# A windowed-attention block on one core: FC2 in three float16 products, with gelu's output split on GpSimd

## The reference

```python
f = _ln(x.transpose(0, 2, 3, 1), g1, b1)
f = jnp.roll(f, (-SS, -SS), axis=(1, 2))
q, k, v = split(_window_partition(f) @ w_qkv + b_qkv)
attn = softmax(einsum('bhid,bhjd->bhij', q, k) * scale + mask)
out = einsum('bhij,bhjd->bihd', attn, v) @ w_proj + b_proj
f = residual + roll_back(_window_reverse(out))
m = _ln(f, g2, b2)
m = gelu(m @ w_fc1 + b_fc1, approximate=False) @ w_fc2 + b_fc2
return f + m
```

## Time and profile before

| | |
|---|---|
| median of 3 runs | 2974.03 us (2972.49 to 2977.97) |
| the profiled execution | 2974.94 us, span 2973.1 us |
| mean granted TensorE clock | 0.99 of full speed |
| busy: TensorE, VectorE, ScalarE, GpSimd | 96%, 81%, 69%, 59% |
| DMA | 359.65 MB, mean 121 GB/s |

### The profile page before, as it was taken

The page is one execution under the profiler, slowest core; times in us unless marked ns, Lnnn a source line. Parts: engine busy times, 40 slices in busy tenths (PEclk is TensorE's granted clock), DMA queues, the critical chain, the costliest instruction groups (busy, mean ns, idle before and its releaser), DMA issues.

```text
span 2973.1 us, 141485 instructions
## 1 busy us (share of the span) xinstructions
PE 2851.0 (96%) x54820; PEld 2383.1 (80%) x54820; DVE 2405.7 (81%) x7142; ACT 2036.8 (69%) x3208; POOL 1760.3 (59%) x2088
## 2 busy tenths in 40 slices
PE   3899999999999999999999999999999999999998
PEld 2788888888878888888887888888888788888886
DVE  6788887888888888788887888888888888888885
ACT  1677776677667777667766776767777677777674
POOL 3566566556656556565665566566565566666655
PEclk7999999999999999999999999999999999999999
DMA  3444444444445444444444444444444444444441
GB/s 72 126 123 126 130 121 126 121 125 126 126 118 130 125 129 123 120 125 123 125 129 114 124 127 125 125 123 125 130 122 126 121 124 130 127 121 129 122 113 42
DMA packets 414934, 359.65 MB, mean 121 GB/s; under 512 B 63646, under 2 KB 414176, under 8 KB 414204
## 3 DMA queue, kind: packets, MB, share of 16 engines
q1 hardware_dynamic: 414220, 350.04, 45.1%
HBM read 193.29 MB, written 154.14 MB: 117 GB/s over the span
## 4 chain that ended last, share of the span: by engine, by line
PE 89%; ACT 5%; issue 3%; DVE 2%; SPq 0%; DMA 0%; POOL 0%; DVEq 0%; POOLq 0%; ACTq 0%
PE psum L502 18%; PE psum L484 10%; PE psum L417 8%; PE psum L466 8%; PE psum L528 7%; PE psum L543 6%; PE psum L618 5%; PE psum L619 5%; PE psum L591 5%; PE psum L424 5%; ACT probs L678 4%; PE psum L428 3%; PE psum L581 3%; PE psum L445 2%; PE psum L570 1%
## 5 line engine op out<-in xcount | busy, mean ns | idle before, releaser
L678 ACT ACTIVATE probs<-psum 113x784 f32<-113x784 f32 x768 | 633.0, 824 | 639.1 <-PE psum L484 635.8
L796 DVE TENSOR_REDUCE nmax<-psum 113x16 f32<-113x784 f32 x768 | 745.5, 971 | 152.0 <-PE psum L466 151.6
L380 POOL TENSOR_SCALAR ve<-mv 98x8 f32<-98x8 f32 (+1 forms) x264 | 64.1, 243 | 1118.7 <-DVE mv L825 1085.9
L502 PE MATMUL psum<-vbd,probs 128*49 128x18 f32 x24576 | 642.5, 198 | 3.7 <-issue 3.0
L502 PEld LDWEIGHTS psum<-vbd,probs 128*49 128x49 f32 x24576 | 632.5, 126 | 6.7 <-issue 6.1
L387 POOL TENSOR_TENSOR rs<-ve,half 98x8 f32<-98x8 f32 (+1 forms) x264 | 435.3, 1649 | 0.0
L484 PE MATMUL psum<-qbd,kst 128*49 128x196 f16 x6144 | 401.5, 251 | 32.9 <-DVE xfl L831 21.9
L392 POOL TENSOR_TENSOR xn<-xn,rs 98x768 f32<-98x768 f32 (+1 forms) x264 | 383.3, 1452 | 74.5 <-POOL rs L387 74.5
L820 DVE BATCH_NORM_STATS2 st<-tok 98x6 f32<-98x96 f32 x2080 | 359.5, 246 | 71.3 <-ACT tok L685 56.4
L466 PE MATMUL psum<-kbd,qst 128*49 128x196 f16 x6144 | 399.2, 250 | 10.6 <-DMA kbd<-stack_pages 7.1
L383 POOL TENSOR_TENSOR xn<-tok,mv 98x768 f32<-98x768 f32 (+1 forms) x264 | 384.8, 1458 | 0.6 <-POOL ve L380 0.6
(11 more groups left out here) (90 smaller groups left out, 5716.3 us busy)
## 6 DMA issues: line engine op xcount, KB each, us to landing
stack_pages<-nat SPq DMA_DIRECT2D x256, 294.0 KB, 3.0
kst<-stack_pages SPq DMA_DIRECT2D x256, 220.5 KB
qbd<-stack_pages SPq DMA_DIRECT2D x1024, 55.1 KB
stack_pages<-nat SPq DMA_DIRECT2D x256, 147.0 KB, 2.1
xr<-in_x_dram SPq DMA_DIRECT2D x224, 147.0 KB, 3.2
out_dram<-yr SPq DMA_DIRECT2D x224, 147.0 KB, 2.3
qst<-stack_pages SPq DMA_DIRECT2D x256, 73.5 KB
kbd<-stack_pages SPq DMA_DIRECT2D x1024, 18.4 KB
```

The costliest lines, as they stand in the source:

```text
L502: last = nc.tensor.matmul(dst[:, :, h, :], probs[:, b.c % 2, h // 4, p, h % 4 * L:(h % 4 + 1) * L], vbd[:, b.c % 4, p * NH + h, :, :], sta ...
L678: nc.scalar.activation(probs[0:PR, b.c % 2, u, :, :].rearrange("j (g q) k -> j g (q k)", g=2), psum[0:PR, B:B + 2, 0:2 * CH], ACT.Exp).the ...
L796: nc.vector.tensor_reduce(dst, psum[0:PR, A:A + 2, 0:2 * CH].rearrange("i g (q h j) -> i g q h j", q=2, j=L), axis=AX.X, op=ALU.max, negat ...
```

## The change

FC2 becomes three float16 products for each float32 one: w2 times 64 is split once into w2h and w2l on VectorE (`split_w2`), the output of gelu is split into hidh and hidl for every band on GpSimd (`split_hidden`, a cast and a subtraction), at the head of the even step. FC2's sum, still in banks D, is read by ScalarE (`scaled`, at the end of its even step), which removes the 64 and adds FC2's bias, into a new tile ys in SBUF; VectorE's `result` adds f to ys, no longer to PSUM. `add_bias` goes. In FC1 the 128-column products of both bands come first (`most`), then the 64-column products of both (`rest`), and `back` in the odd step waits for the first gelu only. In SyncE's queue the high parts are stored at the head of the next step, the maxima after them, and the low parts behind the keys and the results.

```diff
--- before
+++ after
@@ -140,6 +139,9 @@
         oT = sb("oT", [FULL, TOK])
         f = sb("f", [C, 8, TOK])
         hid = sb("hid", [FULL, 2, 3, PART])
+        hidh, hidl = sb("hidh", [FULL, 2, 3, PART], F16), sb("hidl", [FULL, 2, 3, PART], F16)
+        w2h, w2l = sb("w2h", [FULL, 3, C], F16), sb("w2l", [FULL, 3, C], F16)
+        ys = sb("ys", [C, 2, TOK])
         yr = sb("yr", [C, 2, WS, SIDE])
 
@@ -304,13 +307,16 @@
                 alone(sp)
                 sp.dma_start(qbd[MAXROW:MAXROW + 1, n, :, :], mrow[:, n, :]).then_inc(max_in[n], 16)
 
-            def save_parts(b):
+            def save_high(b):
                 n = b.c % 4
                 wait(sp, stack_in[n], b.step(-4).used(4, STACK_IN))
                 alone(sp)
                 sp.wait_ge(qk_high, b.count(1, 1))
                 alone(sp)
                 sp.dma_start(high_parts[n], nat[:, n, 0:4:2, :]).then_inc(high_out[n], 16)
+
+            def save_both(b):
+                n = b.c % 4
                 sp.wait_ge(qk_low, b.count(1, 1))
                 alone(sp)
                 sp.dma_start(both_parts[n], nat[:, n, :, :].rearrange("c (s m) t -> c s m t", s=2)).then_inc(nat_out[n], 16)
@@ -326,14 +332,14 @@
                     key_mask_rows()
                 if first(t, -STACK):
                     stack_mask_rows()
-                for offset, stage in ((LOAD, load_x), (KEYS, key_blocks)):
+                for offset, stage in ((QK - 1, save_high), (LOAD, load_x), (SCORE - 1, maxima), (KEYS, key_blocks)):
                     if has(t.step(offset)):
                         stage(t.step(offset))
                 if odd(t):
                     for offset in STORE:
                         if has(t.step(offset)):
                             store_y(t.step(offset))
-                for offset, stage in ((STACK, stacks), (SCORE, maxima), (QK, save_parts)):
+                for offset, stage in ((QK - 1, save_both), (STACK, stacks)):
                     if has(t.step(offset)):
                         stage(t.step(offset))
 
-                    pool.wait_ge(consts_in, 16 * N_CONST)
-                pool.wait_ge(t_made, b.step(AFTER).count(1, 1))
+            def split_hidden(b):
+                n = b.c % 2
+                pool.wait_ge(gelu_done, b.count(1, 1))
+                wait(pool, fc2_made, b.count(1, -1))
                 alone(pool)
-                nc.gpsimd.tensor_scalar(f[:, b.c % 8, :], f[:, b.c % 8, :], vec[:, BF:BF + 1], None, ALU.add).then_inc(f_biased, 1)
+                nc.gpsimd.tensor_copy(hidh[:, n, :, :], hid[:, n, :, :]).then_inc(hid_high, 1)
+                pool.wait_ge(hid_high, b.count(1, 1))
+                alone(pool)
+                nc.gpsimd.tensor_tensor(hidl[:, n, :, :], hid[:, n, :, :], hidh[:, n, :, :], ALU.subtract).then_inc(hid_low, 1)
 
             def normalise(b):
                 n, groups = b.c % 2, kinds(b) * PAIRS
@@ -394,14 +402,16 @@
 
             def step(t):
                 filling = t.i is None and t.c < 0
+                if not odd(t):
+                    for offset in RESULT:
+                        if has(t.step(offset)):
+                            split_hidden(t.step(offset))
                 if filling and has(t.step(ORDER)):
                     order_x(t.step(ORDER))
                 if turns(t.step(TURN)):
                     normalise(t.step(TURN))
                 if not filling and has(t.step(ORDER)):
                     order_x(t.step(ORDER))
-                if has(t.step(BIAS)):
-                    add_bias(t.step(BIAS))
 
             steps(pool, step)
@@ -417,13 +427,20 @@
                     last = nc.tensor.matmul(dst, weights, tokens[:, b.c % 4, kind, :], start=n == 0, stop=n == 2)
                 return last
 
-            def most_and_rest(bank, high, low, b, kind):
-
-                products = ((high, xfh), (high, xfl), (low, xfh))
-                for n, (weights, tokens) in enumerate(products):
-                    nc.tensor.matmul(three_parts(bank)[:, 0:2, :], weights[:, 0:FULL], tokens[:, b.c % 4, kind, :].rearrange("c (s t) -> c s t", s=2),
-                                     start=n == 0, stop=n == 2)
-                for n, (weights, tokens) in enumerate(products):
+            def products(high, low):
+
+                return enumerate(((high, xfh), (high, xfl), (low, xfh)))
+
+            def most(bank, high, low, b, kind):
+
+                for n, (weights, tokens) in products(high, low):
+                    last = nc.tensor.matmul(three_parts(bank)[:, 0:2, :], weights[:, 0:FULL], tokens[:, b.c % 4, kind, :].rearrange("c (s t) -> c s t", s=2),
+                                            start=n == 0, stop=n == 2)
+                return last
+
+            def rest(bank, high, low, b, kind):
+
+                for n, (weights, tokens) in products(high, low):
                     for s in range(2):
                         last = nc.tensor.matmul(psum[REST * s:REST * (s + 1), bank + 1, 0:PART], weights[:, FULL:FULL + REST], tokens[:, b.c % 4, kind, s * PART:(s + 1) * PART],
@@ -514,7 +531,7 @@
                     pe.wait_ge(f_made, before.count(1, 1))
                 if odd(t):
                     if has(t.step(STORE[1])):
-                        pe.wait_ge(y_made, t.step(STORE[1]).count(1, 1))
+                        pe.wait_ge(y_scaled, t.step(STORE[1]).count(1, 1))
                     else:
                         wait(pe, tokens_in, b.count(1))
                 else:
@@ -534,7 +551,7 @@
                     return
                 pe.wait_ge(normed, b.count(1, 1))
                 if odd(t):
-                    wait(pe, gelu_done, t.step(HIDDEN[1]).count(1, 1)) if has(t.step(HIDDEN[1])) else None
+                    wait(pe, gelu_done, t.step(HIDDEN[0]).count(1, 1)) if has(t.step(HIDDEN[0])) else None
                 if has(t.step(PROB)):
                     pe.wait_ge(exp_done, t.step(PROB).count(QUADS, QUADS))
                 wait(pe, n_low, b.count(1))
@@ -600,23 +617,30 @@
                         pe.wait_ge(exp_done, t.step(PROB).count(QUADS, QUADS))
                 elif has(t.step(SCORE)):
                     pe.wait_ge(s_maxed, t.step(SCORE).count(QUADS, QUADS))
-                last = most_and_rest((B, A)[n], w1h, w1l, b, 1)
-                last.then_inc(fc1_made, 1)
+                most((B, A)[n], w1h, w1l, b, 1)
+
+            def expand_rest(t, n):
+                b = t.step(HIDDEN[n])
+                if has(b):
+                    rest((B, A)[n], w1h, w1l, b, 1).then_inc(fc1_made, 1)
 
             def contract(t, n):
                 b = t.step(RESULT[n])
                 if not has(b):
                     return
+                pe.wait_ge(hid_low, b.count(1, 1))
                 if n == 0:
-                    pe.wait_ge(gelu_done, b.count(1, 2))
                     if turns(t.step(TURN)):
                         pe.wait_ge(tokens_in, t.step(TURN).count(1, 1))
                     else:
-                        wait(pe, y_made, b.count(1))
+                        wait(pe, y_scaled, b.count(1))
+                if first(b, 0):
+                    pe.wait_ge(w2_wide, 2)
                 for s in range(2):
                     dst = psum[0:C, D + n, s * PART:(s + 1) * PART]
-                    nc.tensor.matmul(dst, w2[:, 0, :], hid[:, b.c % 2, s, :], start=True, stop=False)
-                    last = nc.tensor.matmul(dst, w2[:, 1 + s, :], hid[:, b.c % 2, 2, :], start=False, stop=True)
+                    for k, (weights, part) in enumerate(((0, s), (1 + s, 2))):
+                        for m, (w, h) in enumerate(((w2h, hidh), (w2h, hidl), (w2l, hidh))):
+                            last = nc.tensor.matmul(dst, w[:, weights, :], h[:, b.c % 2, part, :], start=k + m == 0, stop=k == 1 and m == 2)
                 last.then_inc(fc2_made, 1)
 
             def step(t):
@@ -633,6 +657,8 @@
                     turn(t)
                     expand(t, 0)
                     expand(t, 1)
+                    expand_rest(t, 0)
+                    expand_rest(t, 1)
                     max_transpose(t)
                     out_transposes(t)
                     back(t)
@@ -717,7 +743,16 @@
                 b = t.step(HIDDEN[n])
                 at = (B, A)[n]
                 act.wait_ge(fc1_made, b.count(1, 1))
+                wait(act, hid_low, b.count(1, -1))
                 nc.scalar.activation(hid[:, b.c % 2, :, :], three_parts(at), ACT.Gelu, scale=1 / GAIN).then_inc(gelu_done, 1)
+
+            def scaled(t, n):
+                b = t.step(RESULT[n])
+                if first(b, 0):
+                    act.wait_ge(consts_in, 16 * N_CONST)
+                act.wait_ge(fc2_made, b.count(1, 1))
+                wait(act, y_made, b.count(1, -1))
+                nc.scalar.activation(ys[:, b.c % 2, :], psum[0:C, D + n, 0:TOK], ACT.Identity, bias=vec[:, BF:BF + 1], scale=1 / GAIN).then_inc(y_scaled, 1)
 
             def step(t):
                 def run(offset, stage, *more):
@@ -747,6 +782,8 @@
```

(14 more changed lines are left out.)

7 lines of the change are left out of this document (3 added, 4 removed).

## The result

| | before | changed |
|---|---|---|
| median, measured together | 2976.0 us (4 runs, 2972.5 to 2979.8) | 2999.8 us (4 runs, 2997.2 to 3002.5) |
| ratio to before, 95% interval | | 1.0082 [1.0066, 1.0097] |
| span of the profiled execution | 2973.1 us | 2997.3 us |
| mean granted TensorE clock | 0.99 | 0.987 |

The forecast was 2859 us. The case that I thought likeliest, no collision and a gain of 115 us, did not come.

A forecast was written before the change was run, and what follows sets the result against it. TensorE's order of products was taken to bound the kernel (89% of the chain). FC2's 0.65 and back's 0.25 us make 0.90 us per pair, times 128 is 115 us: 2859 us by the median, range 2828 to 3060.

The forecast's parts named there:

- The case that I thought likeliest: Whole kernel: no collision of VectorE and GpSimd, 0.90 us saved per pair, 2859 us (2828 to 2890); chance 0.48.
- VectorE's result additions keep their count; only their source moves ... Cost 0 by itself.: VectorE's result: additions wait for ScalarE, ready about 1.9 us into FC2's group and used at 3.0; cost 0.
- Rival 2: VectorE's second result alone is held by GpSimd's product: 0.87 us per pair reaches TensorE, 2971 us; chance 0.17.
- rival 1: VectorE's results and GpSimd lock each other out, both held: 1.3 to 2.2 us per pair, 3026 to 3142 us; chance 0.22.
- FC2 was mis-sized: FC2 on TensorE, from first product to the next group: 2.75 us falls to 2.10, saving 0.65 us per pair.
- "Cost and gain 0" for SP's order: SP's queue: reordered stores and maxima neither cost nor gain, bounded by the 7.1 us key blocks held TensorE up.
- the product's pace: FC2 on TensorE: each float16 product of 196 columns takes 0.083 us, 24 of them, with the change of weights hidden.
- `back` earlier in the odd step: TensorE's odd step: back waits only for the first gelu, 0.25 us saved per pair, bounds 0.05 and 0.45.
- nothing to be had from regrouping FC1: FC1 on TensorE: the second band's wait for the third maxima eats the saving; counted 0, upper bound 0.19 us.
- the split's duration: GpSimd's split: cast about 0.75 us, subtraction 1.15 to 1.2, both bands 4.4 us.
- ScalarE's scaling, 0.58 us each: ScalarE: two ACTIVATEs under 0.66 us each fit an idle stretch of 2.11 us ahead of the next exp; cost 0.
- the margin of 0.5 us: GpSimd's split of the second band is ready 0.5 us before FC2 needs it; cost 0, but thin.

The follow-up runs named there:

- e1: Changed kernel with ScalarE scaling FC2's sum in place in PSUM and VectorE's result reading PSUM and f: 2922.2 us, 0.9816 of the kernel before.
- e11: e1 with ScalarE making the high part of the normalised tokens (xfh) ahead of that of queries and keys in the even step: 2887.6 us, 0.9697.
- e12: e1 with two products instead of three in FC2, the one with the weights' low part left out: 2958.4 us, 0.9938.
- e8: Kernel before with only FC1's products regrouped and back waiting for the first gelu only: 2937.1 us, 0.9877.
- e9: e1 with SP's (SyncE's) queue back in the order of before: 2942.8 us, 0.9906 of the kernel before.
- e10: e1 with FC1 band by band again, back still waiting for the first gelu only: 2913.1 us, 0.9802.
- e13: e1 with FC1 band by band, xfh made first on ScalarE and a loop body of 64 steps: 2839.0 us, 0.9534.
- e14: e13 without a loop, all steps written out: 2840.6 us, 0.9545 of the kernel before.

## Why the prediction was wrong

**The step that failed: "VectorE's result additions keep their count; only their source moves ... Cost 0 by itself."** The source was the point. The second result takes 1.2 us longer beside GpSimd's product and copy, and 0.60 us of it shows as idle time ahead of the third scores, 0.78 from start to start. Reading PSUM instead (e1) brings 0.66 us per pair back. Rival 2 named this mechanism, its place and that it would cancel the gain, and priced it at 0.87 us per pair and 2971 us; the ordinary pairs did come out equal, 22.31 and 22.32. That it cancelled so exactly is luck: its stall was smaller than priced, and so was FC2's gain. I gave it 0.17, and rival 1, the same lock with both results held, 0.22. The collision was written down with its times in both, and the rows of VectorE and GpSimd already overlapped; only the fact that such an overlap costs was missing from the trace.

The Trainium skill stated it (SBUF — State Buffer, section SBUF: two separate sides): VectorE with two SBUF inputs and GpSimd reading SBUF hold a shared pair of ports exclusively for the whole instruction. The runs bear this out for the product (first piece 1.37 us, 0.50 when free) and the copy (0.79 against 0.49). They don't for the power of 8 elements: a result ran in 0.70 us in the middle of its 1.66.

**FC2 was mis-sized: 0.42 us instead of 0.65.** The products came 0.084 apart, as read from `back`. But I took the next group as free to start. The timeline of VectorE before has a row that says otherwise:

```profile
1510.00 0.97 DVE L831 TENSOR_TENSOR xfl<-psum,xfh 96x784 f16<-96x784 f32 x1 [0.33 <-ACT xfh L690]
```

It ended at 1510.97, and the shifted scores, which need it, began at 1511.51. With 0.26 us from its end to their start (1501.70 to 1501.96) there was room for 0.28. It became 0.42 because `xfl` now ends 2.07 us behind FC2's start and not 2.21. I asked who waits inside the shortened stretch, and not what its end had been hiding. e11 gives the 0.22 back, and e12 shows that shortening FC2 further brings nothing while `xfl` stays where it is.

**Missing from the sum: the loop's jump back.** Six jumps cost 23.8 us before and 46.6 now, which is all of the measured difference. I read one typical pair and multiplied by 128. That holds only if the other pairs change by as much. Where the extra time goes is seen, in the second stall, the late table load and the clock; what in the change makes them is open. They came neither with FC1's part (e8 has a second stall of 0.33 and 0.56 us at two jumps and none elsewhere), nor with SP's order (e9), nor with FC2's third product (e12). Left are the split on GpSimd, ScalarE's scaling and the lengths of their instruction streams; none was tried alone. That the time lies inside the range is no merit of the sum: no case had this term.

**"Cost and gain 0" for SP's order was wrong too**, on the other side: with e1's pairs it is worth 20 to 27 us (e9). I had bounded it by the 7.1 us for which the key blocks held TensorE up, and 8.6 us of it lie in the fill, which I didn't read.

**Right:** the product's pace (0.084 us against 0.083); `back` earlier in the odd step (with the regrouped products 0.27 us per pair in e8, 0.25 forecast); nothing to be had from regrouping FC1, since the second band waits for the third maxima (e10); the split's duration (0.67 and 1.30 us, 4.26 for the pair of bands where 4.4 was forecast) and that it is in time; ScalarE's scaling, 0.58 us each, in its idle stretch. The subtraction's 1.30 is nearer to the estimate that I had worked out from the Trainium skill (GPSIMD Engine Reference, section Elementwise — side-by-side cycle accounting), 1.3 to 1.45, than to my own 1.15 to 1.2; the margin of 0.5 us held that.

With each term as measured, the sum closes. The changed kernel is 141 us above the forecast: 85 by the collision (0.66 x 128, e1), 29 by FC2 (0.65 - 0.42 = 0.23 x 128) and 23 at the jumps, 137. From the changed kernel to e13 it is 1.02 us per pair, 131 us over 128, and 27 us at the jumps: 158 of the 161 us measured.

## What to carry to other kernels

Before a VectorE operand moves from PSUM to SBUF, so that both inputs lie there, lay the instruction's start and end beside those of GpSimd's; where they overlap, reckon that it takes longer, as it did here beside a product and a copy and did not beside a power of 8 elements. Leave one input in PSUM or move the operation, and look at what it then delays. When a group on the critical engine gets shorter, ask of the instruction behind it which inputs had come just ahead of its old start: only the distance to the latest of them can be gained. And look at every period of a looped kernel, not at one: where the body jumps back, stalls can cost more than the change is worth, and a longer body removes most of them.

## What was not expected of the hardware

A jump back of a loop costs 4 to 5 us in the kernel before and its two variants and 8 to 10 in the others, with a body of 32 steps as with one of 64. Part of it is the granted clock: in the changed kernel, behind idle stretches of 2.60 and 2.02 us, it was 0.50 for some 10 us. In the kernel before, it stayed at 1.00 behind single stretches of 2.00, 2.22 and 2.44 us of idle, and fell behind those of 2.69, 3.07 and 3.23; the pairs were 24.5 to 24.7 us long where it stayed and 26.5, 30.3 and 27.0 where it fell.

Code without any jump is not free either: in e14 each pair is 0.14 us longer than the same work in a loop. And with fewer products on TensorE (e12) there were stalls of about 1 us at a granted clock of 1.00 for which the profile names no cause. What makes these two is open.
